# Latent attention with four heads to a TensorE round, and a conditioning unit computed two stages earlier

## What is computed

```python
def bi_wkv(r, k, v, w, u, time_emb):          # the conditioned input; k = v = f, r = x
    ...
    num = nf + nb - ekv + euk * vf            # nf, df forward scans, nb, db backward scans over t
    den = df + db - ek + euk
    base = sigmoid(r) * (num / maximum(den, 1e-08))
    return base * (0.8 + 0.2 * tf)

def L1_attn(x, W_dq, W_uq, q_ln_g, q_ln_b, W_dkv, W_ukv, kv_ln_g, kv_ln_b, W_o):
    H, dh = 16, 16
    cq = layernorm(x @ W_dq, q_ln_g, q_ln_b)          # 64 latent channels
    Q = cq @ W_uq
    ckv = layernorm(x @ W_dkv, kv_ln_g, kv_ln_b)      # 64 latent channels
    K, V = split(ckv @ W_ukv)
    q, k, v = ... # [B, H, S, dh]
    scores = where(causal, q @ k.T / sqrt(dh), -inf)
    attn = softmax(scores)
    return (attn @ v).reshape(B, S, D) @ W_o.T

x = x + L0_attn(bi_wkv(x, f, f, L0_cond_w, ...))
x = x + L0_ffn(bi_wkv(x, f, f, L0_cond2_w, ...))
x = x + L1_attn(bi_wkv(x, f, f, L1_cond_w, ...))
x = x + L1_ffn(bi_wkv(x, f, f, L1_cond2_w, ...))
```

## Time and profile before

| | us |
|---|---|
| three runs | 1353.88, 1358.41, 1358.80 (median 1358.41) |
| profiled execution, its time | 1354.94 |
| profiled execution, its span (first to last instruction) | 1353.0 |
| 16 experts, weight tiles of both pairs, in the trace | 404.5 to 664.9 |
| latent attention, in the trace | 664.9 to 857.8 |

### The profile page before, as it was taken

How to read it: one execution, slowest core, us unless ns; L and a number is a source line. 1 busy time by engine, 2 the same in 40 slices (tenths; PEclk the granted TensorE clock), 3 DMA queues, 4 the chain that set the end, 5 groups by cost and what they waited for, 6 DMA issues and landing times. The chain is left out here.

```text
span 1353.0 us, 16485 instructions
## 1 busy us (share of the span) xinstructions
PE 1173.0 (87%) x4614; PEld 625.6 (46%) x4614; DVE 832.0 (61%) x1308; ACT 599.0 (44%) x1747; POOL 425.1 (31%) x467
## 2 busy tenths in 40 slices
PE   0379996999959999999779989787998879988998
PEld 0145542455434444444346556434863338743443
DVE  7799986999856542544368597397521985314222
ACT  4255654555523222422266476475742757510110
POOL 0426562366710000000027265276520765300000
PEclk9989999999969999999989999897997989988999
DMA  6000000000340000000300000300000000000000
GB/s 270 23 1 1 1 1 1 0 0 0 128 168 0 0 0 1 0 0 35 129 27 2 0 0 0 148 1 1 1 1 1 0 0 0 0 8 0 0 0 31
DMA packets 5490, 33.32 MB, mean 25 GB/s; under 512 B 528, under 2 KB 1936, under 8 KB 3536
## 3 DMA queue, kind: packets, MB, share of 16 engines
q1 hardware_dynamic: 5424, 32.61, 6.2%
HBM read 31.56 MB, written 1.05 MB: 24 GB/s over the span
## 5 line engine op out<-in xcount | busy, mean ns | idle before, releaser
L1395 POOL TENSOR_TENSOR prob_latent<-prob_latent,inverse_latent 128x128 f32<-128x128 f32 (+1 forms) x128 | 87.2, 704 | 370.5 <-DVE inverse_latent L1385 370.1
L812 POOL TENSOR_TENSOR decays<-decays,scores 128x768 f32<-128x768 f32 x64 | 119.8, 1874 | 137.8 <-ACT decays L747 137.6
L1985 POOL TENSOR_TENSOR f_pair<-m,weights 128x256 f32<-128x256 f32 x80 | 90.9, 1156 | 94.8 <-DVE m L2006 93.7
L580 PE MATMUL pg<-h,weights 128*128 (+1 forms) x136 | 66.8, 615 | 56.9 <-PEq L359 54.1
L1093 PE MATMUL ph<-h,weights 128*128 x256 | 115.4, 595 | 0.0
L747 ACT ACTIVATE decays<-pcum,neg_cum 128x256 f32<-128x256 f32 (+1 forms) x256 | 86.2, 425 | 7.1 <-PE pcum L633 6.8
L1150 ACT ACTIVATE up<-ph 128x512 f32<-128x512 f32 x44 | 26.3, 597 | 140.6 <-PE ph L1093 140.6
L1235 DVE TENSOR_TENSOR mid<-up,ph 128x512 f32<-128x512 f32 x44 | 30.2, 687 | 93.9 <-ACT up L1150 93.9
L880 DVE SCALAR_TENSOR_TENSOR conv<-px,pp,conv 128x510 f32<-128x510 f32 (+2 forms) x102 | 75.9, 744 | 18.4 <-ACT conv L719 16.0
L580 PE MATMUL px<-h,weights 128*128 x136 | 72.3, 657 | 14.2 <-DVE conv L880 14.2
L1395 POOL TENSOR_TENSOR prob_gqa<-prob_gqa,inverse_gqa 128x128 f32<-128x128 f32 (+1 forms) x128 | 62.1, 506 | 58.6 <-DVE inverse_gqa L1385 56.9
(11 more groups left out here) (328 smaller groups left out, 2783.4 us busy)
## 6 DMA issues: line engine op xcount, KB each, us to landing
weights<-in_w_mixer SPq DMA_DIRECT2D x2, 2048.0 KB, 18.2
weights<-in_w_moe SPq DMA_DIRECT2D x2, 1536.0 KB, 8.2
moe_rest<-in_w_moe SPq DMA_DIRECT2D x2, 1536.0 KB, 13.4
weights<-in_w_gqa SPq DMA_DIRECT2D x1, 3072.0 KB, 10.0
weights<-in_w_gqa SPq DMA_DIRECT2D x1, 2048.0 KB, 14.5
weights<-in_w_moe SPq DMA_DIRECT2D x1, 1920.0 KB, 8.5
weights<-in_w_mixer SPq DMA_DIRECT2D x1, 1536.0 KB, 12.0
weights<-in_w_moe SPq DMA_DIRECT2D x1, 1152.0 KB, 12.5
```

What stands on the lines that cost most here:

```text
L580: op = nc.tensor.matmul(out[0:m, :], w[:, col + k * m:col + (k + 1) * m], net.h[:, ds(i * PAIR + k * TOK, TOK)], start=(k == 0), stop=(k = ...
L812: nc.gpsimd.tensor_tensor(decays[:, head % 4], decays[:, head % 4], scores[:], ALU.mult).then_inc(decay_scaled, 1)
L1395: op = nc.gpsimd.tensor_tensor(self.prob[:, slot, cols], self.prob[:, slot, cols], self.inverse[:, slot, t:t + 1].to_broadcast([P, P * (t ...
L1985: op = nc.gpsimd.tensor_tensor(out[:, :, s, :], src[:, :, 1 - s, :], sin[:, None, s, :].to_broadcast([P, 4, HALF]), ALU.mult)
```

## The change

*In the 16 experts:* a second `CondUnit` (unit 3) runs behind unit 2. For each pair the DVE list is 72 steps, taken 3 to a tile instead of 2. Its ACT calls stand behind the silu of tiles 13 and 14. It writes its factor not to `net.m` but to a buffer that `stage_gqa` reads later (`net.kept`, made of the memory of `f_pair` and `euk`).

*In the latent attention:* no conditioning unit is left in the stage. The mean is taken out of the down projection's weights (DVE, three small operations on 128x256 weights), the projection gives channels on partitions at once, the squares are summed over each half of the channels by a matmul with a matrix of ones (`halves`), and ACT makes the inverse root by Ln and Exp on 128x512. Queries and keys get 32-row slots, 16 rows of a head and 16 rows of zeros, so that four heads fill 128 partitions; the query weights are 64 rows and lie on partitions 0 to 63, the key weights on 64 to 127. The loop is unrolled into 16 rounds, one for each sequence and group of four heads. A round does: four score matmul groups, each on its own 32 rows and its own PSUM bank; the maximum of all four heads on DVE by two reductions; one pass of two transposes that brings the negative maximum to the query's layout (into a row that the zero padding leaves free; the same row of the keys is one); one DVE addition that puts it into the query; the scores again, turned (keys as the stationary operand), two heads at a time; Exp on ACT of 2x384 columns straight into the buffer that the mix reads; the mix of four heads, each on its own 32 columns; a matmul that spreads the row totals (a column of ones in the values gives them), whose inverse ACT makes by Ln and Exp; and one DVE product. POOL only fills constants at the start. The output projection of the first pair and that of the second follow behind the rounds.

```diff
 class CondUnit:
-    def __init__(self, net, c, sems, bounded=None, inverted=None):
+    def __init__(self, net, c, sems, bounded=None, inverted=None, dest=None):
+        self.dest = dest or (lambda pair: net.m[:, ds(pair * PAIR, PAIR)])
 ...
 def stage_moe(net, cfg, weights, prepare, cond, later=(0, ())):
-        unit = CondUnit(net, cond, net.cond_sems) if cond is not None else None
+        units = [CondUnit(net, c, net.cond_sems, dest=d)
+                 for c, d in zip(conds, (None, net.kept))]
+        SECOND = 12
 ...
-                    if m == 1 and unit:
-                        unit.scalar_operands(i, i + turn0)
-                    if m == 2 and unit:
-                        unit.scalar_exp(i + turn0)
+                    for n, unit in enumerate(units):
+                        if m == 1 + n * SECOND:
+                            unit.scalar_operands(i, turn(i, n))
+                        if m == 2 + n * SECOND:
+                            unit.scalar_exp(turn(i, n))
 ...
-                    take(steps, 2)
+                    take(steps, 3)
 ...
 def stage_latent_attention(net):
-        att = Attend(net, mem, "_latent", A_HEADS, P // SLOT, rows_of, pp[0], 4)
+        ps, pst = bank("ps_latent", GROUP), bank("pst_latent", 2)
+        po, aux = bank("po_latent"), bank("aux_latent")
 ...
+            def score(r):
+                g, at = place(r)
+                pe.wait_ge(max_ready, r)
+                for h in range(GROUP):
+                    nc.tensor.matmul(two_diagonals(scores[:, h]), ident, mask, start=True, stop=False)
+                for n, (t, key) in enumerate(((0, 0), (1, 0), (1, P))):
+                    for h in range(GROUP):
+                        rows = rows_of(h)
+                        op = nc.tensor.matmul(scores[:, h, n * P:(n + 1) * P],
+                                              query[g][rows, at + t * P:at + (t + 1) * P],
+                                              keys[rows, g, at + key:at + key + P], start=False,
+                                              stop=(n == 2))
+                op.then_inc(s_ready, 1)
+            def score_turned(r, half):
+                pe.wait_ge(shifted_ready, r + 1)
+                pe.wait_ge(exp_ready, 2 * r + half)
+                for h in range(2):
+                    nc.tensor.matmul(two_diagonals(scores_t[:, h]), ident, mask, start=True, stop=False)
+                for n, (key, t) in enumerate(((0, 0), (0, 1), (P, 1))):
+                    for h in range(2):
+                        ...
+            def mix(r):
+                for t, (a, b) in enumerate(((0, SEQ), (SEQ, TRI))):
+                    for h in range(GROUP):
+                        op = nc.tensor.matmul(po[rows_of(h), t * P:SEQ], values[:, at // P + t, g * GROUP + h, :],
+                                              probs[:, r % 2, h, a:b], start=(t == 0), stop=(t == 1))
 ...
+            for r in range(ROUNDS):                       # PE
+                if r + 1 < ROUNDS:
+                    score(r + 1)
+                score_turned(r, 0)
+                if r >= 1:
+                    mix(r - 1)
+                if r >= 2:
+                    spread_total(r - 2)
+                score_turned(r, 1)
+                if r + 1 < ROUNDS:
+                    turn_max(r + 1)
+            project_out(0, 0)
+            mix(ROUNDS - 1)
+            spread_total(ROUNDS - 2)
+            project_out(0, 1)
+            spread_total(ROUNDS - 1)
+            for k in range(KT):
+                project_out(1, k)
 ...
+            for r in range(ROUNDS):                       # ACT
+                exponential(r, 0)
+                if r >= 1:
+                    take_o(r - 1)
+                if r >= 2:
+                    log_total(r - 2)
+                exponential(r, 1)
+                if r >= 2:
+                    invert(r - 2)
 ...
+            for r in range(ROUNDS):                       # DVE
+                shift(r)
+                if r + 1 < ROUNDS:
+                    maximum(r + 1)
+                if r >= 3:
+                    normalise(r - 3)
 ...
 def stage_gqa(net):
-        tanh_h, make_h, h_ready = condition_input(net, "_gqa")
+        tanh_h, make_h, h_ready = condition_input(net, "_gqa", net.kept)
```

More of the change, by code:

```diff
@@ L127, in __init__ @@
         self.sem = sem
+        self.kept = lambda pair: self.spare[:, ds(pair * UNIT, PAIR)]
         self.stage, self.named = 0, 0
@@ L1248, in _ @@
                 link = Links(dve, links, i, per)
-                steps = unit.vector(link, i, i + turn0) if unit else []
+                steps = [step for n, unit in enumerate(units)
+                         for step in unit.vector(link, i, turn(i, n))]
                 for m in range(N):
@@ L1481, in stage_latent_attention @@
[L1481 to L1490, removed]
@@ L1491, in stage_latent_attention @@
-        o_projected, x_added = sem("o_projected"), sem("x_added_latent")
-        links, once = sem("latent_links"), sem("latent_once")
-        unit = CondUnit(net, 3, net.cond_sems)
+        down = sb("down", [P, KT * 2, LATENT])
+        down_mean = sb("down_mean", [P, KT * 2])
+        slots = sb("slots", [P, A_HEADS, SLOT])
+        halves = sb("halves", [P, P])
+        pick_total = sb("pick_total", [P, GROUP, SLOT])
+        one_row = sb("one_row", [P, 1])
+        keys = sb("keys", [P, A_GROUPS, PAIRS * TOK])
@@ L1514, in _ @@
                                           start=(k == 0), stop=(k == KT - 1))
-            op.then_inc(down_ready, 1)
+                op.then_inc(down_ready, 1)
+            pe.wait_ge(pool_once, 4)
             for pair in range(PAIRS):
[L1517 to L1523, removed]
+                pe.wait_ge(squared, pair + 1)
+                nc.tensor.matmul(p_var[pair], halves[:], square[:, pair * TOK:(pair + 1) * TOK],
+                                 start=True, stop=True).then_inc(var_ready, 1)
@@ new lines, in _ @@
+            for n in range(2):
+                pe.wait_ge(taken[n], PAIRS * USES // 2)
+            pe.wait_ge(pool_once, 8)
+            score(0)
+            turn_max(0)
+            for r in range(ROUNDS):
[9 more added lines that the diff above has]
+                    turn_max(r + 1)
@@ new lines, in _ @@
+            act.wait_ge(net.latent_loaded, 16)
+            for rows, at, scale in ((slice(0, LATENT), WA_Q, A_HEAD ** -0.5),
+                                    (slice(LATENT, P), WA_K, 1.0)):
+                nc.scalar.activation(slots[rows, :, 0:A_HEAD],
+                                     w[rows, at:at + D].rearrange("p (h d) -> p h d", d=A_HEAD),
+                                     ACT.Copy, scale=scale).then_inc(slots_made, 1)
+            toks = [slice(pair * TOK, (pair + 1) * TOK) for pair in range(PAIRS)]
@@ new lines, in take_values @@
+            def take_values(pair, half, engine_op):
+                n = pair * BB * ST + 2 * half
+                out = ring[(pair * USES + 2 * A_GROUPS + half) % len(ring)]
+                return engine_op(values[:, n:n + 2, :, 0:A_HEAD],
+                                 out.rearrange("p (n h d) -> p n h d", n=2, d=A_HEAD))
+            for pair in range(PAIRS):
+                for g in range(A_GROUPS):
+                    use = pair * USES + 2 * g
+                    act.wait_ge(projected, use + 1)
+                    nc.scalar.copy(query[g][:, toks[pair]], ring[use % len(ring)]) \
+                        .then_inc(taken[0], 1)
+                act.wait_ge(projected, pair * USES + 2 * A_GROUPS + 1)
+                take_values(pair, 0, nc.scalar.copy).then_inc(taken[0], 1)
@@ new lines, in exponential, with take_o @@
+            def exponential(r, half):
+                act.wait_ge(st_ready, 2 * r + half + 1)
+                act.wait_ge(mixed, max(r - 1, 0))
+                nc.scalar.activation(probs[:, r % 2, 2 * half:2 * half + 2, :],
+                                     scores_t[:, :, 0:TRI], ACT.Exp).then_inc(exp_ready, 1)
+            def take_o(r):
+                g, at = place(r)
+                act.wait_ge(mixed, r + 1)
+                nc.scalar.copy(o[g][:, at:at + SEQ], po[:, 0:SEQ]).then_inc(o_taken, 1)
```

389 lines of the change are left out of this document (220 added, 169 removed).

## The result

The changed kernel takes **1298.59 us** (median; 1293.68 to 1303.76) beside 1356.14 us for the kernel before on the same chip: a ratio of 0.9576, 95% interval 0.9531 to 0.962. 1287 us was forecast, in a range of 1270 to 1346: the sign, the mechanism and most of the size came as predicted, and 11.6 us of the gain did not come.

A forecast was written before the change was run, and what follows sets the result against it. PE was taken to set the pace. Latent stage 26.6 + 75.6 + 17.7 = 119.9 us for 192.9 (-73.0), experts +0.3, clock +5.2: 1354.9 - 67.5 = 1287 us, range 1270 to 1346.

The forecast's parts named there:

- Tiles side by side: Latent rounds on PE: row tiles (scores) and column tiles (mix) run at once; scores 0.66, turned 1.32, mix 0.65 us.
- Experts at nothing: Expert tiles: the added conditioning unit hides behind PE; +0.3 us, up to +6 if every triple with scans made PE wait.
- A round: Latent attention, four heads of one sequence: PE's list sums to 4.94 us, against 8.9 before.
- the price of a change of tile shape: PE's list in a round: seven changes at 0.10 us, 0.70 in all; between 0 and this for row tiles.
- The clock: Latent stage: two stretches of halved PE clock, 6.9 and 3.5 us, charged again; +5.2 us, between 0 and this.
- Opening: Latent stage before the rounds, with down projection, normalisation, pair projections, first scores and maxima; 26.6 us.
- end: Latent stage behind the rounds: first pair's output projection, last mix and totals, final chain and addition; 17.7 us.
- The rounds in all: Latent attention's 16 rounds: 79.0 us, less 3.4 for parts missing in the first and last, 75.6 us.
- Row tiles in turn: Rival for scores and projections: row tiles don't run side by side; 1347 us, chance 0.10.
- all fours in turn: Rival for scores and mix: neither row nor column tiles overlap in fours; 1378 us, slower; chance 0.05.
- two at a time: Rival for scores and mix: only two tiles run at once, +21 us; 1308 us, chance 0.10.
- PE waiting for the emptying of PSUM: Rival in the rounds: turned scores' single buffer makes PE wait for Exp; 1322 us at worst, chance 0.15.

The follow-up runs named there:

- heads_in_turn: Changed kernel with only the order of score matmuls changed, each head's three behind one another instead of heads alternating; 1335.46 us, ratio 0.9857.
- masks_together: Changed kernel with the first turned half's two masks issued right behind the four score masks; 1294.64 us, ratio 0.9557.
- combined_cut: Kernel combined, with the turned scores' masks taken off PE and multiplied onto the exponentials on POOL and DVE; 1269.24 us, ratio 0.936.
- The fills: Changed kernel plus six unread matmuls in the first round's PE waits, 1289.78 us; with seven more in the opening's waits, 1286.23 us.
- exp_twice: Changed kernel with each Exp of the turned scores computed twice, once into a buffer nobody reads; 1305.89 us, ratio 0.9642.
- no_score_masks: Changed kernel without the four mask matmuls ahead of a round's scores, which only the maximum reads; 1292.95 us, ratio 0.954.
- combined: Changed kernel with six and seven unread matmuls in PE's waits, and without the four score masks a round; 1279.34 us, ratio 0.9435.

## Why the prediction was right, and where its size was off

**Tiles side by side: right.** The point on which the sum turned held for four row tiles, two row tiles and four column tiles. Scores 0.89 us with their change of shape, against 0.66 + 0.10 forecast; a turned half 0.87 against 0.66 + 0.10; the mix 0.79 against 0.65 + 0.10. Twelve such matmuls on the whole array would be 12 x 0.22 = 2.64 us, so four row tiles gave 2.64/0.89 = 3.0 times. The Trainium skill ("TensorE: Matmul & The Clock Gate", Part 3, Measured speedup vs the span model) has 3.07 for four row tiles with 512 columns, and the number of this trace, for 128, is near it. Here it is the change of tile shape that keeps it from 4: behind the first step a group of four records costs 0.112 us, as much as one record on the whole array. heads_in_turn (2.64/1.86 = 1.4 times) shows that the gain depends on the order.

**Experts at nothing: right.** Within a pair the tiles stay 5.37 us apart, all but the first, with DVE at 89.98 instead of 65.11 us; the addition to x starts at 663.40 as in the earlier trace rows. Neither the +0.3 nor the +6 showed.

**A round: 5.38 for 4.94, the first mis-sized term.** The term is the price of a change of tile shape, of which the forecast took 0.10 us to be the upper bound. From start to start the steps without any change come to 4.18 us, 4.24 in the sum, and the extra time ahead of the first matmul of a new shape to 0.70 for the seven changes, as in the sum. What it lacked is that the first step behind a change is longer too: a first score record lasts 372 ns against 270 for the later ones, and the next one starts 0.21 us behind it, not 0.11. Three changes into row tiles and the one into the spread of the totals (0.10 each) and smaller ones for turning (0.06), mix (0.03) and masks (0.01) make 0.50 us, the 0.44 by which the round is longer and the 0.06 saved in the steps: **7 us** in sixteen rounds. A change of tile shape costs up to 0.2 us in all, not 0.10; masks_together and combined_cut show it from the other side.

**The clock: the second mis-sized term.** I charged two stretches, 6.9 + 3.5 us, at half: 5.2. The rounds got 3.4 + 20.5 us of it, which costs 12 us. It stands behind the waits of 2.0 and 1.0 us in the first round: the first of them I had put into the opening as mere length, and for the second, where mix and total are missing, I had taken time off the round without asking what PE does meanwhile. I had named a halved clock in the rounds as what would spoil the forecast and gave it no price. The fills show that this idle time is a condition of it; that it is the whole cause is not shown.

**The rest.** Opening 27.3 for 26.6, end 18.2 for 17.7. The rounds in all (692.2 to 787.3) took 95.1 us; forecast were 75.6 and the 5.2 of clock, so they are 14.3 too long, 7.0 by the round and 6.8 by the clock. With 0.7 and 0.5 that is 15.5 us. The stages behind gave 3.9 back (805.5 to the end 491.3 us, from 857.8 in the kernel before 495.2) at a granted clock that happened to be higher, and the experts did not take their 0.3: 11.3, beside the 11.2 by which 1298.6 lies above the sum's unrounded 1287.4. The 3.9 us are luck: without them the time would be 1302.5, still inside the range, but above the 1270 to 1300 that had been given 0.58.

**The rivals.** Row tiles in turn, all fours in turn, and two at a time are refuted by the timeline of the round. PE waiting for the emptying of PSUM did not come, but it was near: mix and total with their changes, 1.28 us in the forecast, take 743.73 - 742.40 = 1.33, and some 0.34 us are to spare, as exp_twice bears out. The Trainium skill's rule that emptying PSUM may become the limit of a tiled kernel ("TensorEngine Tiling (Array Packing)", Performance Considerations, PSUM Bottleneck) did not decide this one; masks_together and exp_twice show such a wait, of 0.27 and some 0.5 us a round, once the cover is a little thinner or the emptying longer.

**Still open:** why the halved stretch, once begun, lasts 20.5 us of uninterrupted PE work in two traces of the changed kernel, 34.1 in heads_in_turn, 23.9 in no_score_masks and 3.4 in masks_together and exp_twice.

## What to carry to other kernels

Where heads are narrow, give each its own 32 rows and issue neighbouring matmuls on different rows: the order of two loops was worth 1.6 us of a round of 5.4. Count the changes of tile shape, at up to 0.2 us each, and what stands between a PSUM bank's last matmul and its next use, before moving work on PE. Fill PE's waits at the head of a dense stage: six matmuls that nobody reads gave back 9 us.

## What the runs showed of the hardware that was not expected

An f32 matmul of 128 columns leaves two records here, 0.11 us apart, and the pace of tiles side by side is set by these, not by matmuls. Between two heads in turn the next head's first record starts 0.33 us behind the former's first, ahead of that head's last ones, so part of the overlap survives even a bad order.

DVE's product of two 256-column tiles takes longer while POOL multiplies. In combined (first fence) POOL has nothing to do; in combined_cut it does (second, POOL and DVE; its last line is a product of the last rounds that falls beside no work of POOL's):

```profile
734.95 0.41 DVE L1840 TENSOR_TENSOR decay<-decay,inverse_latent 128x256 f32<-128x256 f32 x1
```

```profile
734.13 1.27 POOL L1520 TENSOR_TENSOR probs<-probs,keep 128x512 f32<-128x512 f32 x1 [2.95 <-ACT probs L1738]
734.57 1.11 DVE L1857 TENSOR_TENSOR den<-den,inverse_latent 128x256 f32<-128x256 f32 x1
...
753.95 0.42 DVE L1857 TENSOR_TENSOR e_pair<-e_pair,inverse_latent 128x256 f32<-128x256 f32 x1
```

0.41 or 0.42 against 1.11 us: a transfer of work to POOL is paid in part by DVE.
